# Cross attention rewritten head by head: 97-row score matmuls, keys stored per batch, one pipeline over all eight blocks

## The reference, cut to what matters

```python
x = x + linear_attention(layernorm(x))
x = x + cross_attention(layernorm(x), ctx)
x = x + experts(layernorm(x))

def cross_attention(query, ctx):          # 16 heads of 32
    q, k, v = proj(query, Wq, bq), proj(ctx, Wk, bk), proj(ctx, Wv, bv)
    scores = einsum('bhqd,bhkd->bhqk', q, k) / sqrt(32)
    attn = softmax(scores)                # over 154 keys
    return einsum('bhqk,bhkd->bhqd', attn, v) @ Wo.T + bo
```

## Time and profile before

| what | value |
|---|---|
| median of 3 runs | 2717.04 us |
| the profiled execution | 2708.45 us, span 2706.6 us |
| TensorE busy | 2575.7 us, 95% |
| VectorE / ScalarE / GpSimd busy | 1307.0 / 884.7 / 355.3 us |
| mean granted TensorE clock | 0.974 of full |
| stage `attend_cross`, first DMA to first DMA of `experts` | 767.74 to 1334.09 us |

### The profile page before, as it was taken

One profiled execution on the slowest core, in us unless ns is written; L12 is line 12 of the kernel. 1 busy time (PEld: TensorE's weight loads), 2 busy tenths in 40 slices (PEclk: granted clock), 3 DMA queues, 4 the chain that ended last, 5 costly groups with the idle time before them and its releaser, 6 DMA issues.

```text
span 2706.6 us, 34174 instructions
## 1 busy us (share of the span) xinstructions
PE 2575.7 (95%) x12680; PEld 1938.6 (72%) x12680; DVE 1307.0 (48%) x2027; ACT 884.7 (33%) x1411; POOL 355.3 (13%) x301
## 2 busy tenths in 40 slices
PE   7999997999969998999799999999989999999999
PEld 6888874666645555555478888888877888888887
DVE  5555546676645546564443343433444334433434
ACT  3555566776523332332221212121122121112121
POOL 1444452333410111011000000000000000000000
PEclk9999997999979998999899999999999999999999
DMA  6654554755231212022220000000132000000001
GB/s 191 172 133 125 135 116 123 216 161 153 86 115 55 79 47 79 32 97 90 100 84 24 23 23 23 23 23 23 46 123 87 24 23 23 23 23 23 23 23 62
DMA packets 67779, 207.00 MB, mean 76 GB/s; under 512 B 9968, under 2 KB 11760, under 8 KB 55664
## 3 DMA queue, kind: packets, MB, share of 16 engines
q1 hardware_dynamic: 67376, 204.81, 24.5%
q0 software_dynamic: 288, 0.69, 0.1%
HBM read 122.27 MB, written 58.72 MB: 67 GB/s over the span
## 4 chain that ended last, share of the span: by engine, by line
PE 49%; DMA 1%; DVE 0%; issue 0%; ACT 0%; SPq 0%; DVEq 0%
PE ex_pg L1921 32%; PE ex_pd L1936 16%; DMA stage<-x_scratch 1%; PE ex_pg L1896 0%; DVE ex_x L1849 0%; ACT ex_x L1761 0%; DMA ex_lower<-in_lower 0%; DVE ex_h L1799 0%; DVE ex_s_g L1799 0%; DVE ex_w L1792 0%; PE ex_pd L1906 0%; DVE ex_acc L1842 0%; DVE ex_r_w L1853 0%; ACT ex_r_w L1764 0%; DVE ex_lt L1804 0%
## 5 line engine op out<-in xcount | busy, mean ns | idle before, releaser
L1921 PE MATMUL ex_pg<-ex_x,ex_w 128*128 128x512 f32 x3840 | 887.4, 391 | 3.3 <-DVE ex_lt L1804 3.3
L1921 PEld LDWEIGHTS ex_pg<-ex_x,ex_w 128*128 128x128 f32 x3840 | 724.7, 189 | 154.3 <-issue 3.5
L1936 PE MATMUL ex_pd<-ex_w,ex_ht 128*128 128x512 f32 x1920 | 446.6, 389 | 0.0
L1870 DVE TENSOR_TENSOR ex_h<-ex_s_g,ex_pg 128x512 f32<-128x512 f32 x160 | 110.1, 688 | 650.4 <-PE ex_pg L1921 650.0
L1936 PEld LDWEIGHTS ex_pd<-ex_w,ex_ht 128*128 128x128 f32 x1920 | 360.5, 188 | 74.7
L1777 ACT ACTIVATE ex_s_g<-ex_pg 128x512 f32<-128x512 f32 x160 | 95.8, 599 | 749.1 <-PE ex_pg L1921 748.9
L1842 DVE SCALAR_TENSOR_TENSOR ex_acc<-ex_pd,ex_share,ex_acc 128x512 f32<-128x512 f32 x320 | 234.4, 748 | 90.3 <-PE ex_pd L1936 84.9
L378 POOL TENSOR_TENSOR pr_ks_sum<-pr_ks_sum,pr_kp 128x512 f32<-128x512 f32 x128 | 165.0, 1290 | 166.6 <-DVE pr_kp L501 155.0
L584 PE MATMUL pr_pj<-pr_xt,pr_w 128*128 128x512 f32 x768 | 184.6, 398 | 1.4 <-DVE pr_xt L472 1.4
L584 PEld LDWEIGHTS pr_pj<-pr_xt,pr_w 128*128 128x128 f32 x768 | 145.3, 192 | 31.7 <-DVE pr_xt L472 1.8
L1308 ACT ACTIVATE cr_ring<-cr_s_bank 128x512 f32<-128x512 f32 x160 | 95.8, 598 | 202.4 <-PE cr_s_bank L1532 202.4
(11 more groups left out here) (176 smaller groups left out, 2790.8 us busy)
## 6 DMA issues: line engine op xcount, KB each, us to landing
stage<-in_units SPq DMA_DIRECT2D x21, 1536.0 KB, 6.5
qk<-pr_kq SPq DMA_DIRECT2D x192, 128.0 KB, 2.4
qk<-q_scratch SPq DMA_DIRECT2D x96, 256.0 KB, 4.5
q_scratch<-pr_kq SPq DMA_DIRECT2D x128, 128.0 KB, 2.3
...
```

The source lines that it names most:

```text
L1870: nc.vector.tensor_tensor(h[:, f], s_g[:, f], pg[2 * f + 1][:], ALU.mult).then_inc(h_set, 1)
L1921: mm = nc.tensor.matmul(pg[2 * f + which][:], w[:, slot, sp_, col:col + P], x3[:, m, k, c * TB:(c + 1) * TB], start=(n == 0), stop=(n == 3 ...
L1936: mm = nc.tensor.matmul(pd[t][:], ht[:, s % 2, sp_, f, t * P:(t + 1) * P], w[:, slot, m, WD + f * D:WD + (f + 1) * D], start=(n == 0), sto ...
```

## The change

The linear stage makes both parts of the queries itself. ScalarE writes the HI part, and a new VectorE operation `query` the LO part; a store now carries both. `normalise` of a block is placed in other slots on VectorE.

The cross stage is one pipeline over all 8 blocks, without a loop over batches:

- The keys of both batches have room. Head h has 96 rows: HI, HI and LO of its 32 key rows, against HI, LO and HI of its query rows in `q3`. So one matmul does what three passes did. Row 97 holds -1 in the keys and the row maximum in the queries, so the same matmul subtracts the maximum. SP places the keys with 12 small DMAs and loads the queries with 3 DMAs per group, into a ring of 6 groups. Padding and the row of -1 are memsets on GpSimd.
- The unit of remaining keys is four float32 matmuls of 32 output rows.
- The maxima are made on 96 rows with all 154 keys of a head, so 64 matmuls of 154 columns per block, in 24 jobs. Those of block i+1 stand in turn i, between scores and in the output projection, across batches too. They are turned in float32, and ScalarE sends them with 4 DMAs into row 97.
- The last attention group, the spreading, output projection, norm and transposes of block i-1 are done in turn i.
- The reciprocals are split into HI and LO (ScalarE, GpSimd), and spread in two short passes. GpSimd makes the LO part of `u`, and ScalarE copies the transposes out.
- Keys and values of batch 1 are made in turn 2.

```diff
@@ attend_linear
-                    nc.scalar.activation(xq[:, g % 2], bank_of(m, "XQ", g)[:], ACT.Identity, bias=bq[:, g:g + 1])\
-                        .then_inc(xq_taken, 1)
+                    nc.scalar.activation(xq[:, g % 2, HI], bank_of(m, "XQ", g)[:], ACT.Identity, bias=bq[:, g:g + 1])\
+                        .then_inc(xq_hi, 1)
+                def query(m, g):
+                    dve.wait_ge(xq_hi, G * m + g + 1)
+                    nc.vector.scalar_tensor_tensor(xq[:, g % 2, LO], bank_of(m, "XQ", g)[:], bq[:, g:g + 1],
+                                                   xq[:, g % 2, HI].bitcast(F32), ALU.add, ALU.subtract)\
+                        .then_inc(xq_taken, 1)
@@ attend_cross: the jobs of the three PSUM banks
+    PIECES = [[(t, j) for j in range(3)] for t in range(TT)] + [[(t, 3) for t in range(3)], [(3, 3)]]
+        m = ahead(i, 2)
+        jobs += ahead(i, 0) + one("R", *range(G)) + ahead(i, 1)
+        jobs += m[0:first] + one("O", 0) + m[first:second] + one("O", 1) + m[second:] + ahead(i, 3) + one("O", 2)
+        jobs += [(i + 1, "MT")] if i + 1 < NBLK else []
...
+    JOBS = [key for i in range(NBLK) for key in turn_jobs(i, 2, 5)] + LAST_JOBS
@@ tensor
-                        for c, (s, m) in enumerate(PASSES):
-                            nc.tensor.matmul(s_bank[n % SBANKS][:], k_w[:, s, g, j * P:(j + 1) * P], q[:, m, g],
-                                             start=(c == 0), stop=False)
-                        nc.tensor.matmul(s_bank[n % SBANKS][:], minus[:, n // SU, n % SU], mxt[:], start=False,
-                                         stop=True).then_inc(s_full, 1)
+                    if j < HG:
+                        mm = nc.tensor.matmul(out, k_w[:, i // BLK, g * HG + j, 0:P], q3[:, slot_of(i, g), j], start=True,
+                                              stop=True)
+                    else:
+                        for h in range(HG):
+                            mm = nc.tensor.matmul(out[h * HD:(h + 1) * HD], k_w[:, i // BLK, g * HG + h, P:KW].bitcast(F32),
+                                                  q3[:, slot_of(i, g), h].bitcast(F32), start=True, stop=True,
+                                                  skip_group_check=True)
+                    for at, (t, j) in enumerate(PIECES[n]):
+                        mm = nc.tensor.matmul(bank_of(i, "MX", g, n)[:, at * KEYS:(at + 1) * KEYS],
+                                              q3[0:K3, slot_of(i, g), j, t * P:(t + 1) * P],
+                                              k_w[0:K3, i // BLK, g * HG + j, 0:KEYS],
+                                              start=True, stop=True, skip_group_check=True)
+                def out_tile(i, t, units):
+                    out_proj(i, t, 0, 6)
+                    maxima(units)
+                    out_proj(i, t, 6, 3 * G)
@@ tensor, a turn i
+                        score(i, 0, 0)
+                        score(i, 0, 1)
+                        dens_heads(i - 1, G - 1)
+                        score(i, 0, 2)
+                        score(i, 0, 3)
+                        dens_rest(i - 1, G - 1)
+                        score(i, 0, 4)
+                        nums(i - 1, G - 1)
+                    scores(i, 1, ahead(i, 0))
...
+                    attend(i, 0)
+                    if i:
+                        spread_out(i - 1)
+                    scores(i, 2, ahead(i, 1))
+                    attend(i, 1)
+                    if i:
+                        out_tile(i - 1, 0, m[0:2])
+                        maxima(m[2:3])
+                        out_tile(i - 1, 1, m[3:5])
+                        maxima(m[5:6])
...
+                    scores(i, 3, ahead(i, 3))
+                    if i:
+                        out_tile(i - 1, 2, [])
+                    if i + 1 < NBLK:
+                        turn_maxima(i + 1)
...
+                    if i:
+                        out_tile(i - 1, 3, [])
...
+                        transposes(i - 1, 0)
+                        transposes(i - 1, 1)
+                    attend(i, 2)
...
+                        transposes(i - 1, 2)
+                        transposes(i - 1, 3)
@@ scalar
+                def maxima_out(i):
+                    act.wait_ge(filled, POS[(i, "MT")] + 1)
...
+                    nc.scalar.copy(mxt[:], bank_of(i, "MT")[0:H, :]).then_inc(act_read, 1)
+                    act.wait_ge(act_read, ACT_AT[(i, "MT")])
+                    for g in range(G):
+                        act.dma_start(q3[K3:ROWS, slot_of(i, g)].bitcast(F32).rearrange("p j t -> p (j t)"),
+                                      mxt[g * HG:(g + 1) * HG].bitcast(F32)).then_inc(mx_in, 16)
@@ sync
+                def load_q(i, g):
+                    n = G * i + g
+                    if n >= QRING:
+                        sp.wait_ge(s_full, SU * (n - QRING + 1))
+                    src = xq_dram[i].rearrange("s (j d) (g t) -> s d g j t", j=HG, g=G)
+                    for r, s in enumerate((HI, LO, HI)):
+                        sp.dma_start(q3[r * HD:(r + 1) * HD, n % QRING].bitcast(F32), src[s, :, g]).then_inc(q_in[n % QRING], 16)
```

924 lines of the change are left out of this document (512 added, 412 removed).

## The result

The changed kernel takes 2627.01 us (median of 4 runs, 2626.68 to 2627.39) against 2716.96 us of the kernel before in the same comparison (4 runs, 2706.17 to 2719.36): a ratio of 0.9676, 95% interval 0.9651 to 0.9702. In a later comparison of 5 runs it took 2625.09 us against 2713.36, ratio 0.9675 (0.9661 to 0.9689). The forecast was 2638, range 2608 to 2668. The profiled execution took 2626.68, where 2629 was forecast.

The account below looks back on a forecast made before the run. TensorE, busy 95%, bounds the kernel. A turn of 52.5 us for a block's 60.4 makes the cross stage 486.7 us against 566.4, 79.7 less: 2629 for the profiled execution, 2638 for the median with 8.6 added, range 2608 to 2668.

Parts of the forecast that it names:

- The guess between 0.115 and 0.138: Maxima matmuls of 154 columns on TensorE: 0.126 us each taken, 8.1 us per turn for 64, 2.5 more than before.
- The rival of short matmuls at 0.32 us: Maxima below 256 columns run like plain float32, 12 us more per turn, about 2725 us; chance 0.04.
- The terms of the walk: New waits of TensorE in one turn, walked through once: together 5.2 us, bounds 2 to 9.
- Group 1's 0.6: Scores of group 1: with two score banks and 0.60 us per exponential, TensorE waits 0.6 us.
- Group 2: Scores of group 2: 0.8 us for ScalarE's four casts between exponentials, 0.5 for VectorE's four multiplications holding the banks.
- Tile 1's wait for maximum m2: Output tile 1 wants the bank of m2, which VectorE reads only after m0 and m1: 0.8 us.
- The second maximum for tile 1's bank: In group 3 it waits 1.0 us, as VectorE takes tile 0's moments and m5 before tile 1.
- Fewer waits: Rival: VectorE is ahead at the meetings, a turn is 49.5 us, 21 less in all, 2617 us; chance 0.16.
- more waits: Rival: bank order and VectorE's order clash in every group, a turn is 57 us, 2670 in all; chance 0.14.
- the low clock in turn 0: Turn 0, the cross stage's first: 3 us allowed for the low clock within the 37 us forecast.
- The clock rival: Many short waits bring the clock to 1.2 GHz in score groups and first output tiles: 22 us more per turn, 2790; chance 0.04.
- The linear stage: VectorE's 32 new operations, 22 us beside matmuls, change the stage's time by 0, with -8 to +8 us.

Follow-up runs that it names:

- experiment 1: The changed kernel with each of a block's 16 head score matmuls issued four times: 2688.46 us, ratio 0.992 to the kernel before.
- experiment 5: The changed kernel with wide matmuls that nothing reads, 8 ahead of the stage's first maxima and 14 while these are away: 2619.14 us, ratio 0.9656.
- Experiment 10: Experiment 9 plus unread wide matmuls in the waits of turn 7 and the drain, and VectorE's statistics of tile 0 later: 2625.06 us, ratio 0.9682.
- experiment 9: The changed kernel with 8 and 6 unread wide matmuls in the start's waits, block 1's maxima moved forward, last block's low parts before bias: 2621.71 us.
- experiment 7: The changed kernel with GpSimd making the last block's four low parts ahead of its bias additions: 2627.53 us, ratio 0.969.
- Experiment 8: The changed kernel with another order of banks, output tile 1 taking the bank right behind tile 0's: 2644.37 us, ratio 0.9737.
- experiment 4: The kernel before with the changed kernel's linear stage, its cross stage reading only the HI part of the queries: 2712.56 us, ratio 1.0005.
- experiment 2: The changed kernel with the pipeline drained after batch 0 and filled anew for batch 1: 2662.43 us, ratio 0.9825.

## Why the prediction was right, step by step

The direction, the stage and the range hold. The forecast for the stage was 486.7 us; it is 480.8. That the two are so close is in part luck: six turns came out 15 us shorter than forecast, and turn 0, turn 7 and the drain together 11.2 us longer. Of the 11 us between the forecast of 2638 and the median of 2627.01, 8.6 are the step from the profiled execution to the median, read off the kernel before; in the changed kernel the two are 0.3 us apart (2626.68 and 2627.01).

| term, us | forecast | after |
|---|---|---|
| start to first maxima | 24.9 | 21.6 |
| start to first score | 45.8 | 43.7 |
| turn 0 | 37 | 43.25 |
| turns 1 to 6, six turns | 6 x 52.5 | 6 x 50.0 |
| keys and values of batch 1 | 11 | 11.2 |
| turn 7 | 41 | 43.7 |
| drain | 29.5 | 31.8 |
| to the experts' first DMA | 7.4 | 7.2 |

**The turn: 47.3 us of matmuls and 5.2 of waits forecast; 47.8 and 2.2 by the brackets, some 46.9 and 3.1 with the hidden waits.** The matmuls by TensorE's rows, start to start:

- Scores: 7.7 forecast, 9.0 measured. Of these, 0.63 us are the hidden waits in two pairs (0.31 and 0.32), so some 8.3 are matmuls. A pair with nothing in its way takes 0.48 to 0.51 us ahead of maxima, 0.24 to 0.26 a matmul, and 0.58 to 0.75 ahead of the 32-column sets or behind them. The 0.232 of a run of many was a little low for that (experiment 1, where eight stand in a row, has 1.85 to 2.07 us for them, 0.243 each in the mean).
- Maxima: 8.1 forecast, 8.4 measured, 0.3 of it the hidden wait ahead of 1077.44; so 0.126 each with the steps to the wide matmuls around, and 0.105 inside a group of six. The guess between 0.115 and 0.138 was right. The rival of short matmuls at 0.32 us is dead. The sum by the rule on weight loads in the Trainium skill ("TensorE: Matmul & The Clock Gate", LDWEIGHTS and Part 3) was 0.17 us, and this trace does not agree with it.
- Attention: 16 sets at 1.00 forecast, 14.4 measured, since sets that follow one another take 0.86.
- Spreading: 1.9 forecast, 2.2 measured.

**The waits.** The terms of the walk, 0.7 + 0.6 + 0.8 + 0.5 + 0.8 + 1.0 + 0.6, add up to 5.0 and not to 5.2. Four of the seven were well sized. Group 1's 0.6 is there, in no bracket: 0.3 ahead of 1077.44 and 0.3 in that pair. Group 2: 0.8 + 0.5 forecast, 0.7 (0.39, and 0.32 in the pair at 1087.91) + 0.40 measured. Tile 1's wait for maximum m2: 0.8 forecast, 0.73 measured. The others were too large. At the turn's start 0.7 was forecast and no bracket shows any: ScalarE's first exponential begins at 1070.76, 0.8 us into the turn, and the attention matmuls between the scores put the third score off to 1071.60. The second maximum for tile 1's bank: 1.0 forecast, 0.51 measured. Tile 2: 0.6 forecast, 0.15 measured. There the walk had the place and too little of the work that TensorE has in between. "Fewer waits" (a turn of 49.5) came closest by the turn, but the total didn't reach its 2617, because of the next point; "more waits" (57) is dead.

**Turn 0, turn 7, the drain: the step that was too small.** Together 107.5 us forecast, 118.75 measured. I allowed 3 us for the low clock in turn 0. Without its wait for DMAs turn 0 takes 43.25 - 0.68 = 42.6 us with the clock low for most of it, and 34.9 - 3.3 = 31.6 in experiment 5 with the clock up: the term is 11 us. Turn 7 was forecast with 3 us of waits less, and without maxima to fill its scores it has six waits for exponentials of 0.2 to 1.0 us instead, 3.3 us together. In the drain the clock was at 0.50 to 0.83 from 1220 to 1235 us. Experiment 10 kept it at 1.00 and gained 0.2 us there on experiment 9, so the clock weighs little in the drain. The wait of 3.33 us for GpSimd's low parts weighs more: experiment 7 took 2.5 us off it, and as much off the drain.

**The clock rival** was given 0.04, and the changed kernel does not show it in a turn. Experiment 8 does: a reordering of a few matmuls is enough. The Trainium skill names this failure ("TensorE: Matmul & The Clock Gate", A second HAM failure mode), TensorE idling shortly and often while it cycles through PSUM banks. The trace of experiment 8 agrees in kind, the clock being at 0.50 behind short waits for banks. How often TensorE idles does not part the two kernels: experiment 8 has four bracketed waits in a turn, 1.9 us, and the changed kernel five, 2.2 us, with the clock at 1.00. So the kernel's margin against it is thin, and 0.04 was low for it.

**The linear stage** at 0 was right (experiment 4). The new operation is 0.75 us and not 0.69, and TensorE now waits 0.25 and 0.46 us for VectorE where it waited 1.46:

```profile
651.27 1.33 PE L1079 MATMUL li_bank<-li_rec,li_spread 128*128 128x512 f32 x4 [0.25 <-DVE li_xq L983]
...
653.06 3.06 PE L1114 MATMUL li_bank<-li_u_ln,li_wq 128*128 128x512 f32 x12 [0.46 <-DVE li_num L936]
```

**What the gain is made of.** Of the 90 us, 62 to 66 hang on one score matmul for four (experiment 1), 35 to 40 on no drain between the batches (experiment 2). They overlap, so they aren't to be added. The shorter spreading and the output tiles placed behind other work were not taken back by themselves; that they bring something is read from the rows alone (5.0 us from the numerators to the first output matmul before; 2.6 us for the spreading now, 0.40 of it a wait).
